# Turning the probabilities by VectorE block transposes and DMA instead of TensorE, with three smaller edits to the scan of a decoder layer

## The reference

```
x = x + ssm(layernorm(x))              # selective state space, 512 channels, 16 states
x = x + attention(layernorm(x), ctx)   # 32 heads of 128, position bias, mask
x = x + ffn(layernorm(x))              # 512x512 and 16 experts of rank 16

# ssm
xp = x @ x_proj.T                      # dt_in (16), B (16), C (16)
dt = softplus(dt_in @ dt_proj.T + b)
h = exp(dt * A) * h + dt * B * x       # over the 128 positions
y = sum_n h * C + D * x
# attention, for each head
q = rmsnorm(x) * w @ wq.T;  k = ctx @ wk.T;  v = ctx @ wv.T
p = softmax(mask(q @ k.T + bias));  out += (p @ v) @ wo.T
```

## Time and profile before

| what | value |
|---|---|
| median of 3 runs | 911.64 us (909.94 to 913.21) |
| the profiled execution | 913.16 us |
| its span in the trace | 911.3 us |
| busy: TensorE (PE) | 904.1 us, 5150 matmul records |
| busy: VectorE (DVE) | 699.7 us |
| busy: ScalarE (ACT) | 516.7 us |
| busy: GpSimd (POOL) | 667.0 us |
| moved by DMA | 150.26 MB, 165 GB/s over the span |

### The profile page before, as it was taken

The page is one execution under the profiler, slowest core; times in us unless marked ns, Lnnn a source line. Parts: engine busy times, 40 slices in busy tenths (PEclk is TensorE's granted clock), DMA queues, the critical chain, the costliest instruction groups (busy, mean ns, idle before and its releaser), DMA issues.

```text
span 911.3 us, 15431 instructions
## 1 busy us (share of the span) xinstructions
PE 904.1 (99%) x5150; PEld 778.2 (85%) x5150; DVE 699.7 (77%) x761; ACT 516.7 (57%) x1190; POOL 667.0 (73%) x431
## 2 busy tenths in 40 slices
PE   9999999999999999999999999999999999999998
PEld 7687688888888888788899999999899999999876
DVE  5789997999999999556666667676767676767784
ACT  3686858576565575365655555555555555555330
POOL 3246779897758778367698878888988878787522
PEclk9899999999999999999999999999999999999999
DMA  9545566666686754357645454545444445454302
GB/s 310 162 139 175 158 198 194 203 202 196 189 273 198 247 160 169 122 170 228 194 137 158 136 158 135 158 137 160 136 159 135 160 134 168 132 168 137 104 1 93
DMA packets 96850, 150.26 MB, mean 165 GB/s; under 512 B 10577, under 2 KB 35281, under 8 KB 96673
## 3 DMA queue, kind: packets, MB, share of 16 engines
q1 hardware_dynamic: 86432, 131.54, 44.2%
q10 hardware_dynamic: 10368, 18.09, 7.9%
HBM read 113.81 MB, written 35.78 MB: 164 GB/s over the span
## 4 chain that ended last, share of the span: by engine, by line
PE 87%; DVE 10%; issue 1%; DMA 1%; ACT 1%; POOL 0%; DVEq 0%; ACTq 0%; SPq 0%
PE acc L509 11%; PE acc L511 11%; PE acc L510 11%; PE misc L511 6%; PE misc L509 6%; PE misc L510 6%; PE acc L736 6%; PE acc L791 6%; PE acc L668 5%; PE acc L669 5%; PE acc L670 5%; DVE misc L1232 4%; PE acc L760 3%; DVE w L1239 2%; DVE misc L1227 2%
## 5 line engine op out<-in xcount | busy, mean ns | idle before, releaser
L1494 POOL TENSOR_TENSOR y<-y,w 128x2048 f32<-128x2048 f32 x31 | 143.5, 4629 | 58.3 <-DVE w L1239 57.3
L1232 DVE TENSOR_TENSOR_SCAN misc<-dA,misc 128x2048 f32<-128x2048 f32 x32 | 141.7, 4429 | 4.2 <-ACT dA L863 1.0
L1084 ACT ACTIVATE prob<-prob,negm 128x128 f32<-128x128 f32 x256 | 99.9, 391 | 43.7 <-DVE negm L1302 43.7
L1091 ACT ACTIVATE ot_hi<-acc 128x512 fp32r<-128x512 f32 x64 | 38.3, 598 | 143.0 <-PE acc L791 143.0
L1555 POOL TENSOR_TENSOR wt_lo<-ws,wt_hi 128x1024 fp32r<-128x1024 f32 x27 | 65.0, 2408 | 61.0 <-ACT wt_hi L1072 58.9
L509 PE MATMUL misc<-wo_hi,ot_hi 128*128 128x512 f32 x256 | 107.1, 418 | 0.0
L511 PE MATMUL misc<-wo_hi,ot_lo 128*128 128x512 f32 x256 | 101.3, 396 | 0.0
L509 PE MATMUL acc<-wv_hi,ctx_hi 128*128 128x512 f32 x256 | 101.0, 395 | 0.0
L510 PE MATMUL misc<-wo_lo,ot_hi 128*128 128x512 f32 x256 | 100.8, 394 | 0.0
L1572 POOL TENSOR_TENSOR wo_lo<-wo_raw,wo_hi 128x512 fp32r<-128x512 f32 x64 | 95.7, 1495 | 6.2 <-ACT wo_hi L1048 6.2
L510 PE MATMUL acc<-wv_lo,ctx_hi 128*128 128x512 f32 x256 | 99.9, 390 | 0.0
(11 more groups left out here) (198 smaller groups left out, 2448.9 us busy)
## 6 DMA issues: line engine op xcount, KB each, us to landing
k_scratch<-kst SPq DMA_DIRECT2D x64, 256.0 KB, 3.5
bc<-xp_scratch ACTq DMA_DIRECT2D x32, 512.0 KB, 5.8
v_scratch<-vst SPq DMA_DIRECT2D x32, 512.0 KB, 4.0
k_sb<-k_scratch SPq DMA_DIRECT2D x64, 256.0 KB, 2.7
v_sb<-v_scratch SPq DMA_DIRECT2D x64, 256.0 KB, 2.6
wo_raw<-in_wo SPq DMA_DIRECT2D x64, 256.0 KB, 2.9
wp<-in_wq SPq DMA_DIRECT2D x54, 256.0 KB, 3.7
wraw<-in_wk SPq DMA_DIRECT2D x32, 256.0 KB, 5.1
```

The costliest lines, as they stand in the source:

```text
L1084: last = act.activation(prob[q][:, b], prob[q][:, b], ACT.Exp, bias=negm[q][:, b:b + 1], accum_out=psum[q][:, b:b + 1])
L1232: dve.tensor_tensor_scan(h_ps, flat(dA[k % 2][:, :, :, :]), h_ps, 0.0, ALU.mult, ALU.add).then_inc(da_free, 1)
L1494: pool.tensor_tensor(y_half(half), y_half(half), w[:, k % 2], ALU.add).then_inc(y_ready, 1)
```

## The change

There are four edits.

1. The probabilities are turned in another way. VectorE transposes the 32x32 blocks of `prob` into `blocks` (`turn`, one STREAM_TRANSPOSE for a head), SP writes these to DRAM (`p_scratch`), waits, and reads them back by four DMAs with the block rows and columns exchanged, in rows of 512 bytes. TensorE's transposes and VectorE's COPY go away. PV comes a step later and in the middle of the step, the output products too, and W12 is put ahead of S2.
2. z of the first half is normalised on ScalarE (`z_norm_0`), not on VectorE after round 26.
3. Exponentials are put ahead of the logarithms: at `LOG_AT` those of all rounds to 11, and in the first half the logarithm ahead of a key copy; the copy of B for round 1 comes earlier.
4. The second half's dt projection is one fp32r pass over 96 rows (three groups of 16 that hold high and low parts, `dtw3` and `xp3`) in the place of a product in fp32.

```diff
-HOOKS = (24, 26)
-T_SUM, T_TR, T_XP, T_DT, T_EXP = 273, 45, 340, 85, 234
+HOOK = 24
+T_SUM, T_TR, T_XP, T_DT, T_EXP = 273, 45, 340, 23, 234
...
@@ SP, step
+                if runs(g - 2):
+                    sp.wait_ge(blocks_out[p], in_count(g - 2, p, 16))
+                    for k in range(4):
+                        sp.dma_start(pt_sb[p][32 * k:32 * (k + 1), :, :, :].rearrange("j q b i -> j q (b i)"),
+                                     p_dram[p, :, :, k].rearrange("q j x -> j q x")).then_inc(pt_in[p], 16)
                 if runs(g) and runs(g + 1):
                     if not known(g) or g >= 1:
                         sp.wait_ge(sb_done, g)
                     load_kb(g + 1, head(g + 1, half), 1 - p)
...
+                    sp.wait_ge(turned, g)
+                    sp.dma_start(p_dram[1 - p].rearrange("q j k x -> (q j) k x"),
+                                 blocks[1 - p][:, :, :, :].rearrange("p k b i -> p k (b i)")).then_inc(blocks_out[1 - p], 16)
...
@@ TensorE
-                return pe.matmul(out, dtw[:, c * P:(c + 1) * P], xp_sb[0:R, half], start=True, stop=True)
+                cols = slice(c * P, (c + 1) * P)
+                if half:
+                    return pe.matmul(out, dtw3[0:R3, cols], xp3[0:R3], start=True, stop=True)
+                return pe.matmul(out, dtw[0:R, cols], xp_sb[0:R, 0], start=True, stop=True)
...
                 elif paired(i) and not p:
+                    pe.wait_ge(s1_done, count(i))
+                    product(sumX, W12, pp, *z_of(half, 1, 0), False).then_inc(p2_done, 1)
                     pe.wait_ge(wc_lo, count(i))
                     if not known(i) or i > FIRST_PAIR:
                         pe.wait_ge(c21_done, count(i) - 1)
                     product(sumY, S2, pp, *t_of(half, T2), True).then_inc(p6_done, 1)
-                    pe.wait_ge(s1_done, count(i))
-                    product(sumX, W12, pp, *z_of(half, 1, 0), False).then_inc(p2_done, 1)
...
-                if runs(g - 2):
-                    pe.wait_ge(p_ready, g - 1)
...
-                    for b in range(HB):
-                        mm = pe.transpose(psT[:, b * S:(b + 1) * S], prob[p][:, b], ident[:])
-                    mm.then_inc(t_done, 1)
...
                 if runs(g - 3):
+                    pv(g - 3, 1 - p)
+                if runs(g - 4):
...
+            def pv(h, p):
+
+                pe.wait_ge(pt_in[p], in_count(h, p, 64))
+                pe.wait_ge(v_in[p], in_count(h, p, 16))
...
+                    pe.wait_ge(ot_lo_done, h)
+                for b in range(HB):
+                    mm = pe.matmul(psO[:, b * S:(b + 1) * S].rearrange("p (q i) -> p q i", q=4), v_sb[p][:, b],
+                                   pt_sb[p][:, :, b], start=True, stop=True)
+                mm.then_inc(pv_done, 1)
@@ ScalarE
-            k_copy(0, 7)
             act.wait_ge(sp_exp, 2)
             act.activation(u[:, 0], w[:, 0], ACT.Ln, bias=1.0).then_inc(sp_log, 1)
+            k_copy(0, 7)
...
+            def z_norm_0(b):
+
+                act.wait_ge(ln_root, 3)
+                act.wait_ge(z_bias_done, 1)
+                act.activation(y_tok[:, b], base[:, b], ACT.Identity, scale=rstd[:, 1, b:b + 1],
+                               bias=z_bias[:, b:b + 1]).then_inc(zn0_done, 1)
...
-                    if s != LOG_AT + 1:
+                    if s == LOG_AT:
+                        emitted = exps(emitted, 11 * C)
+                    elif s != LOG_AT + 1:
                         emitted = exps(emitted, due(s))
@@ VectorE
-                if k == HOOKS[1]:
-                    z_norm(0)
...
-                if runs(g - 2):
-                    dve.wait_ge(t_done, g - 1)
-                    if not known(g) or g > 3:
-                        dve.wait_ge(pv_done, g - 3)
-                    dve.tensor_copy(pt_sb[p][:, :, :].rearrange("p b q -> p (b q)"), psT).then_inc(pt_evac, 1)
...
+            def turn(h, q):
+
+                dve.wait_ge(p_ready, h + 1)
+                if not known(h) or h >= 2:
+                    dve.wait_ge(blocks_out[q], in_count(h - 2, q, 16))
+                dve.transpose(blocks[q][:, :, :, :].rearrange("p k b i -> p b k i"),
+                              prob[q][:, :, :].rearrange("p b (k j) -> p b k j", j=32)).then_inc(turned, 1)
```

More of the change, by code:

```diff
@@ L50 @@
 B_AT = 2
+R3 = 96
+ZN_AT = 3
 ENTRY = 12
@@ L90, in due @@
     e = EARLY + sum(single.get(t, T_SUM) for t in range(XT[0] + 1, s)) // T_EXP
-    return min(C * NSTEP, e - sum(e > C * k for k in HOOKS))
+    return min(C * NSTEP, e - (e > C * HOOK))
 EXP_AT = DT[-1] + 2
@@ L140, in decoder_layer @@
         h_ps = misc[:, :, :].rearrange("p c t -> p (c t)")
+        with ExitStack() as proj:
+            xp_sb = sb(proj, "xp_sb", [P, 2, HT])
+            xp3 = sb(proj, "xp3", [P, HT], F32R)
+            dtw3 = sb(proj, "dtw3", [P, D], F32R)
         base = sb(whole, "base", [P, B, D])
@@ L203, in decoder_layer @@
         prob = [sb(whole, f"prob{i}", [P, HB, S]) for i in pair]
-        pt_sb = [sb(whole, f"pt_sb{i}", [P, HB, S]) for i in pair]
+        pt_sb = [sb(whole, f"pt_sb{i}", [P, 4, HB, 32]) for i in pair]
         bm = [sb(whole, f"bm{i}", [P, HB, S]) for i in pair]
@@ L208, in decoder_layer @@
         ffn_w = sb(whole, "ffn_w", [P, C, D])
-        o_sum = sb(whole, "o_sum", [P, 2, D])
+        blocks = [sb(whole, f"blocks{i}", [P, 4, HB, 32]) for i in pair]
+        o_sum = ea_sb
         with ExitStack() as second_raw:
@@ L296, in decoder_layer @@
         mx_done, exp_done, rec_done = sem("mx_done"), sem("exp_done"), sem("rec_done")
-        p_ready, t_done, pt_evac, pv_done = sem("p_ready"), sem("t_done"), sem("pt_evac"), sem("pv_done")
+        p_ready, turned, pv_done = sem("p_ready"), sem("turned"), sem("pv_done")
+        blocks_out, pt_in = [sem(f"blocks_out{i}") for i in pair], [sem(f"pt_in{i}") for i in pair]
         ot_hi_done, ot_lo_done, o_done, x2_done = sem("ot_hi_done"), sem("ot_lo_done"), sem("o_done"), sem("x2_done")
@@ L329, in pipeline @@
                     step(4 * i + p, p, 0, 2 * i + p // 2)
-            for g in range(H - 4, H + 4):
+            for g in range(H - 4, H + 8):
                 step(g, g, g // H, g // 2)
                 behind(g)
-            with eng.Fori(H // 4 + 1, STEPS // 4 - 1) as i:
+            with eng.Fori(H // 4 + 2, STEPS // 4 - 1) as i:
                 for p in range(4):
                     step(4 * i + p, p, 1, 2 * i + p // 2)
-            for g in range(STEPS - 4, STEPS + 3):
+            for g in range(STEPS - 4, STEPS + 4):
                 step(g, g, 1, g // 2)
@@ L625, in z_transpose @@
                     if c == 0:
-                        pe.wait_ge(zn_done, half * HB + b + 1)
+                        pe.wait_ge(zn_done if half else zn0_done, b + 1)
                     mm = pe.transpose(out[:, b * S:(b + 1) * S], y_tok[:, half * HB + b, c * P:(c + 1) * P], ident[:])
@@ L786, in step @@
                     v_sum(NG - 1, B - 1)
-                if runs(g - 2):
-                    pe.wait_ge(pt_evac, g - 1)
-                    pe.wait_ge(v_in[p], in_count(g - 2, p, 16))
-                    for b in range(HB):
-                        mm = pe.matmul(psO[:, b * S:(b + 1) * S], v_sb[p][:, b], pt_sb[p][:, b], start=True, stop=True)
-                    mm.then_inc(pv_done, 1)
+            def pv(h, p):
+                pe.wait_ge(pt_in[p], in_count(h, p, 64))
+                pe.wait_ge(v_in[p], in_count(h, p, 16))
+                if known(h) and h == 0:
+                    pe.wait_ge(sum_evac, slot(NG, 0) - 1)
+                else:
+                    pe.wait_ge(ot_lo_done, h)
[3 more added lines that the diff above has]
+                mm.then_inc(pv_done, 1)
             def behind(g):
@@ L903, in exps @@
                         load_bc(k + 1)
-                    if c == B_AT and k:
+                    if c == B_AT and k >= 2:
                         b_copy(k)
@@ L960, in _ @@
             y0_copy(0, range(2, C))
+            b_copy(1)
             emitted = exps(emitted, C + 2)
@@ L970, in xp_slot @@
             def xp_slot():
-                act.activation(xp_sb[0:RX, 1], bank(XP)[0:RX], ACT.Copy).then_inc(sum_evac, 1)
+                r = bank(XP)
+                act.wait_ge(rows_set, 2)
+                act.wait_ge(dtw_in, 16 * 3)
+                act.activation(dtw3[0:R3], dtw[0:R3], ACT.Copy)
+                for i in range(3):
+                    act.activation(xp3[32 * i:32 * i + R], r[0:R], ACT.Copy)
+                act.activation(xp_sb[0:RX, 1], r[0:RX], ACT.Copy).then_inc(sum_evac, 1)
                 act.wait_ge(sum_evac, XP + 1)
@@ L1011, in _ @@
                         yt_slot(j)
+                    if g == 6 and ZN_AT <= j < ZN_AT + HB:
+                        z_norm_0(j - ZN_AT)
                     if g == 6 and KP <= j < KP + C:
@@ L1327, in step @@
                                       ALU.mult).then_inc(p_ready, 1)
+                    if not paired(i):
+                        turn(g - 1, q)
```

134 lines of the change are left out of this document (78 added, 56 removed).

## The result

The changed kernel takes 977.62 us (median of four, 973.42 to 981.64) against 910.79 for the kernel before in the same comparison: ratio 1.073, interval 1.070 to 1.076. It is 7.3% slower, where 889 us was forecast. The profiled execution has a span of 971.6 us; before it was 911.3.

A forecast was written before the change was run, and what follows sets the result against it. TensorE, busy 904.1 of 911.3 us, was taken as the bound. Transposes -28.2, scan -3.8, TensorE held up +5.4, start +2.5 and end +1.3 made -22.8 us: 889 us predicted, range 880 to 906.

The forecast's parts named there:

- The trip by DMA: From `turned` to `pt_in`: write landing taken at 3.0 us, then four reads; 7.1 us against room of 8.0 to 8.7.
- The sum on SP's queue: SP's issues per attention step: landing 3.0, reads 1.9, k and bias 1.0, v and wo 1.0; 6.9 of 7.06 us.
- the trip sets the pace: Rival: SP's queue needs 7.9 us a step at a landing of 4.0, kernel slower at 929 us; 8 in 100.
- The sum for the traffic: DMA in the attention stage: 0.5 MB a step added to 1.1 MB, using 0.75 of the DMA engines.
- transposes off TensorE: Attention: four transposes a head leave TensorE, 0.44 us together, 28.2 us saved over 64 heads.
- scan: Scan stage: 3.3 us from the second dt projection and 0.5 from a TensorE wait, 3.8 us saved.
- TensorE held up in 27 pairs: Attention pairs: VectorE's thin margin and `q_sb` for S2 without PV as cover cost 0.2 us a pair, 5.4 in all.
- start: First attention steps: output products moved out of step 3 leave a hole on TensorE, 2.5 of 2.8 us lost.
- end: Last head: transpose and trip after its `prob` delay TensorE's final PV, costing 1.3 us.
- VectorE's transpose: VectorE in attention: one STREAM_TRANSPOSE a head takes 0.69 us, like the reduction, unstretched by GpSimd.
- The rival of a slow transpose: Rival: VectorE's transpose takes over 0.9 us (893 us at 0.95, 926 at 1.55); 20 in 100, 3 over 1.3.
- What would show it: Expected signs: pairs of 14.3 us, transpose 0.7, landing near 3 us, SP waiting for the transpose; TensorE at `pt_sb` means mis-sized trip.

## Why the prediction was wrong

The step that failed is the landing of the write, taken at 3.0 us in "The trip by DMA"; the changed kernel shows 4.6. The sum on SP's queue was set up rightly there (write, landing, reads, k and bias, v and wo), and with 4.6 in place of 3.0 it is 8.5, over the 7.5 of before. That is the rival "the trip sets the pace", with its place, its queue and its point of decision at 7.6 us; it had been given 8 in 100, and its 929 us assumed a landing of 4.0 at most. Two things were missing, and a third was right.

- *The position in the queue.* The rows that priced the landing were a store with nothing about it (2.0) and the slowest store (4.0). The text noted that v and wo, 0.5 MB, stand ahead of the write, and then took the middle. The queue in fact has k, bias, v, wo and the write within 2 us. In the three orders it lands in 4.6 us right behind the loads, 2.7 at the head of a step, 2.0 ahead of v and wo, and the last of them gives back 77 of the 81 us. Which of its two effects carries this is not separated: with v and wo beside the landing, even 4.6 would make 4.6 + 1.8 + 1.0 = 7.4 (an estimate), just under the 7.5 of before. And the place alone does not make 4.6: where no engine waits, it is 3.5.
- *The same wait decides its own length.* While SP has time, it waits for the transpose, the write comes well behind wo and lands in 2.0 to 3 (run with two reads). The later SP is, the closer it issues the write behind the loads and the longer the landing, up to 4.6. At 4.6 the ring is 8.3 us or more and stays late. So a sum near the limit (6.9 of 7.06, with an end of the range at 7.9) was no case of "it just fits": what SP is late by lengthens its own ring. Both directions are on record: the changed kernel starts in time and is late for good from its fourth write on; the kernel with two reads, whose ring is 7.4 at a landing of 4.6, becomes nearly as late and recovers.
- *The bandwidth* was rightly held not to decide: 231 GB/s cost nothing without the waits. The sum for the traffic, 0.75 of the DMA engines, came out as 0.77 in the kernel with the write ahead of v and wo.

The other terms, by the runs (us; the third column is for the kernel without the trip):

| term | forecast | measured | from |
|---|---|---|---|
| transposes off TensorE | -28.2 | -22.7 | 0.355 a head to the next start |
| scan | -3.8 | -2.8 | scan's edits alone |
| TensorE held up in 27 pairs | +5.4 | +6.5 | 14.55 less 15.02 - 0.71 |
| start | +2.5 | +3.3 | its wait for `ot_lo` there |
| end | +1.3 | +2.3 | last c21 to the end, 52.1 against 49.8 |
| sum | -22.8 | -13.4 | measured as a whole: -14.9 |

- *The transposes* were mis-sized by 5.5 us. The 0.44 comes from a group in the tail, ahead of another kind of product (L681). In 62 of the 64 groups the next start is 0.35 to 0.36 behind the group's, here in the trace of before:

```profile
722.84 0.60 PE L760 MATMUL acc<-ident,prob 128*128 128x128 f32 x4
723.19 0.47 PE L509 MATMUL misc<-wo_hi,ot_hi 128*128 128x512 f32 x1
```

  0.35 us, beside the group's duration of 0.60 with a modelled end. The other 0.08 fit what the output products take longer behind an fp32 group (2.88 against 2.80 us in the kernel with PV at the step's end): PV, in fp32 too, now stands in the transposes' place and keeps it. The distance to the next start had been used rightly for PV, 0.84 from 726.76 to 727.60, beside its duration of 1.05.
- *VectorE's transpose* was right, 0.701 against 0.69 us. The rival of a slow transpose is refuted. From the Trainium skill, "VectorE: DVE Perf Modes", section "The three transpose paths", which gives 311 ns for 128x128 in bf16, 1.24 us had been worked out as an estimate; the trace disagrees, with 0.70.
- *TensorE held up* was right in size, 6.5 against 5.4, and in its kind: a `q_sb` sum that comes late because PV is gone from the step's end. The place was not the one named, so that the size is in part luck. The forecast had c21 before S2, which costs 0.06 us a pair in the kernel without the trip. Most of it is c12 before the odd step's scores: from the start of S3 to the scores it is 0.99 and 1.07 to 1.10 us in turn there, against 0.72 where S4 is early. PV put back alone did not cure it, because then the product `prob<-prob,rec` stands in front of c12 on VectorE.
- *The scan*: its own run gives 2.8, with an interval that holds the 3.8. Between the two profiled executions the first scores are 5.1 us earlier (384.90 against 389.98), but 2.0 of these had arisen before the second dt projection (93.22 against 91.18), the first of TensorE's own instructions that an edit changes. The edits on ScalarE stand ahead of it, so whether they or chance gave the 2.0 is open; the comparison of many executions is the better measure.
- *The start and the end* had the right sign and were each about 1 us short.
- *PV with its runs of 32 columns* costs what it did: 0.81 us to the next start, against 0.80 to 0.84 before.
- *The reads of the trip* took 1.75 us for four issues and landed in 2.0, against 1.9 and 2.7: right or better.
- *What would show it*: the forecast had said that if TensorE stands at `pt_sb`, the trip was mis-sized, and that SP should wait for the transpose and not the other way round. TensorE does stand at `pt_sb`, and SP waits for the landing, never for the transpose: both signs name the step.

## What to carry to other kernels

Where an edit puts a wait for a transfer's landing on a queue that also issues loads, add up the ring of that queue with the landing that the transfer has at its own position, behind the loads issued just before it, and not with that of a lone store; if the sum comes within a tenth of the step (here 6.9 of 7.06), being late can lengthen the landing and keep the queue late, so issue the write ahead of the loads. Price an instruction that leaves a pipelined engine by the distance to the next start in the steady stage, not by its duration or by one group in the tail, and look at what will stand in its place. Where two chains end at the same place, removing one shows nothing: cut both, or cut one at a time in a kernel where the other has been cut.

## What the runs showed of the hardware

- A write of 256 KB from SBUF to DRAM on SP's queue lands in 2.0 us in the median ahead of two loads of 256 KB, 2.7 at the head of a step, and behind the loads in 2.5, 3.5 or 4.6, the longer the closer it follows them (2.0 over 2.7 us behind the last, 4.0 under 1.2 us, in one and the same execution).
- PV's eight fp32 matmuls take 1.08 us to the next start when they sum over 64 rows, and 0.81 over 128: half the rows took longer.
- VectorE's STREAM_TRANSPOSE of 128x512 in fp32 takes 0.70 us, as long as a reduction of the same size, and is not stretched (0.701 and 0.696 on average in two kernels).
- The product of two SBUF tensors on VectorE is held up where GpSimd works beside it, and hardly less when it is short. The page's groups for the same 128x64 elements, in the kernel with PV at the end and in the one with PV in the middle:

```profile
L1351 DVE TENSOR_TENSOR prob<-prob,rec 128x64 f32<-128x64 f32 x51 | 53.4, 1048 | 1.8
```

```profile
L1360 DVE TENSOR_TENSOR prob<-prob,rec 128x64 f32<-128x64 f32 x49 | 17.1, 348 | 1.7
```

  An eighth of the elements takes 1.05 us on average in the one and 0.35 in the other. With all elements the means are 1.42 and 0.83. With no GpSimd instruction beside it the same product takes 0.23 and 0.69 us. So the first kernel adds 0.8 to the short one and 0.7 to the whole, the second 0.1 to each: what it waits goes by its place in time, not by its length. The Trainium skill, "SBUF — State Buffer", section "Who interferes with whom", has the rule that such an instruction contends with GpSimd's; the rows agree, and add that it holds for a short one too.
